# First seven input tiles of a two-layer expert kernel given a place each and issued from two queues

## The reference

```python
# layer 0, on x (8, 256, 1024)
base   = einsum('btd,od->bto', x, W)                    # W (1024, 1024)
logits = einsum('btd,ed->bte', x, Wr) + 5.0 * one_hot(language_ids)   # 8 experts
topw, topi = top_k(logits, 2)
gates  = sum(one_hot(topi, 8) * softmax(topw)[..., None], axis=-2)
h      = einsum('btd,erd->bter', x, A)                  # A (8, 16, 1024)
x      = x + base + 2.0 * einsum('bter,bte,eor->bto', h, gates, B)
# layer 1, on the new x
w      = weight[adapter_ids]                            # weight (16, 1024, 1024)
out    = x + einsum('bsi,boi->bso', x, w)
```

## Time and profile before

| | us |
|---|---|
| median of three runs | 405.21 (404.77 to 405.67) |
| the profiled execution's own time | 404.49 |
| span of the profiled execution | 402.7 |
| TensorE matmul busy | 396.1 (98%) |
| VectorE busy | 313.9 (78%) |
| ScalarE busy | 170.9 (42%) |
| GpSimd busy | 62.9 (16%) |
| DMA moved | 72.79 MB, mean 181 GB/s |

### The profile page before, as it was taken

The page is one execution under the profiler, slowest core; times in us unless marked ns, Lnnn a source line. Parts: engine busy times, 40 slices in busy tenths (PEclk is TensorE's granted clock), DMA queues, the critical chain, the costliest instruction groups (busy, mean ns, idle before and its releaser), DMA issues.

```text
span 402.7 us, 5968 instructions
## 1 busy us (share of the span) xinstructions
PE 396.1 (98%) x1920; PEld 334.6 (83%) x1920; DVE 313.9 (78%) x404; ACT 170.9 (42%) x231; POOL 62.9 (16%) x88
## 2 busy tenths in 40 slices
PE   8999999999999999999999999999998999999996
PEld 8999888888889888888888888888887887888884
DVE  2999999997457468329887958997979999999900
ACT  1443342754220143335355335465445566556511
POOL 1016102200000100000110222312313131314100
PEclk9999999999999999999999999999999999999999
DMA  7978520133376300007595999999999999999231
GB/s 188 232 200 221 151 61 0 53 106 104 115 215 207 92 0 2 1 0 206 127 297 211 311 249 302 266 304 284 261 284 269 286 277 302 292 263 271 66 104 52
DMA packets 78577, 72.79 MB, mean 181 GB/s; under 512 B 7090, under 2 KB 77266, under 8 KB 77522
## 3 DMA queue, kind: packets, MB, share of 16 engines
q1 hardware_dynamic: 51584, 47.21, 46.8%
q10 hardware_dynamic: 26962, 25.21, 19.9%
HBM read 55.61 MB, written 16.78 MB: 180 GB/s over the span
## 4 chain that ended last, share of the span: by engine, by line
PE 98%; issue 0%; POOL 0%; ACT 0%; POOLq 0%
PE banks L1178 15%; PE banks L1180 14%; PE banks L1179 14%; PE banks L1083 13%; PE banks L1081 13%; PE banks L1082 13%; PE banks L1074 7%; PE banks L1062 3%; PE banks L1092 2%; PE banks L1094 2%; PE banks L1093 2%; PE banks L1152 1%; PE banks L1101 0%; ACT sums L959 0%; POOL sums L415 0%
## 5 line engine op out<-in xcount | busy, mean ns | idle before, releaser
L1081 PE MATMUL banks<-ring,weights 128*128 128x512 f32 x192 | 75.0, 391 | 0.0
L427 POOL TENSOR_TENSOR raw<-raw,ident 128x128 f32<-128x128 f32 x50 | 34.9, 698 | 221.6 <-DMA raw<-in_L_cond_weight_dram 198.1
L1178 PE MATMUL banks<-weights,tokens 128*128 128x512 f32 x176 | 68.6, 390 | 0.0
L1180 PE MATMUL banks<-weights,tokens 128*128 128x512 f32 x176 | 68.5, 389 | 0.0
L1179 PE MATMUL banks<-weights,tokens 128*128 128x512 f32 x176 | 68.5, 389 | 0.0
L948 ACT ACTIVATE weights<-weights_f 128x1024 fp32r<-128x1024 f32 x44 | 46.5, 1060 | 50.1 <-DVE weights_f L634 46.5
L634 DVE STREAM_TRANSPOSE weights_f<-raw 128x1024 f32<-128x1024 f32 x42 | 51.8, 1235 | 10.5 <-POOL raw L427 10.0
L640 DVE TENSOR_TENSOR weights<-weights_f,weights 128x1024 fp32r<-128x1024 f32 x44 | 52.6, 1197 | 1.0 <-ACT weights L948 0.9
L1083 PE MATMUL banks<-ring,turned_w 128*128 128x512 f32 x128 | 49.8, 389 | 0.0
L1082 PE MATMUL banks<-tokens,weights 128*128 128x512 f32 x128 | 49.8, 389 | 0.0
L1081 PEld LDWEIGHTS banks<-ring,weights 128*128 128x128 f32 x192 | 36.0, 188 | 7.5
(11 more groups left out here) (116 smaller groups left out, 632.4 us busy)
## 6 DMA issues: line engine op xcount, KB each, us to landing
raw<-in_L_cond_weight_dram SPq DMA_DIRECT2D x168, 128.0 KB, 6.2
ring_f<-in_L_cond_weight_dram SPq DMA_DIRECT2D x88, 128.0 KB, 6.3
raw<-in_x_dram SPq DMA_DIRECT2D x64, 128.0 KB, 3.3
x_kept<-stage ACTq DMA_DIRECT2D x32, 256.0 KB, 4.1
out_dram<-sums ACTq DMA_DIRECT2D x32, 256.0 KB, 7.0
raw<-in_L_cond_W_dram SPq DMA_DIRECT2D x32, 128.0 KB, 3.1
sums<-x_kept ACTq DMA_DIRECT2D x3, 1024.0 KB, 7.4
stage<-x_kept ACTq DMA_DIRECT2D x3, 1024.0 KB, 9.7
```

What stands on the lines that cost most here:

```text
L427: nc.gpsimd.tensor_tensor(spot, spot, ident[:].rearrange("p (q j) -> p q j", q=Q), ALU.add)\
L1081: nc.tensor.matmul(ps, u_hi, x_hi, start=first and k == 0, stop=False, skip_group_check=True)
L1178: nc.tensor.matmul(l1_bank(o), x_hi, w_hi, start=m == 0, stop=False)
L1180: mm = nc.tensor.matmul(l1_bank(o), x_lo, w_hi, start=False, stop=m == M - 1)
```

## The change

`FRONT = 7`: the first seven tiles (A, x0 to x3, W0, W1) get places 0 to 6, of which 0 to 2 are in `raw` and 3 to 6 in `ring_f`. None of them waits. All later tiles of layer 0 go through the three places of `raw`, counted from the eighth tile; the w1 tiles' places are shifted accordingly. The four DMAs of each of the seven tiles are divided: parts 0 and 1 are issued by SyncE, parts 2 and 3 by ScalarE, ahead of, between and behind ScalarE's DMAs of Wr, the language ids and the adapter ids. On VectorE, the low part of W0 comes ahead of the transposition of W1.

```diff
+    FRONT = 7
+    SLOT = {item: k if k < FRONT else (k - FRONT) % RAW for k, item in enumerate(LOADS)}
     for n in range(NW1):
-        SLOT["w1", n] = (N_LOADS + n) % RAW if n < EARLY else (n - EARLY + RAW) % RAW1
+        SLOT["w1", n] = (N_LOADS - FRONT + n) % RAW if n < EARLY else (n - EARLY + RAW) % RAW1
...
+        def fill(engine, item, rows, parts=range(Q)):
+            s = SLOT[item]
+            for c in parts:
+                engine.dma_start(raw_tile(s)[c * S:(c + 1) * S, :].rearrange("p (q j) -> p q j", q=Q),
+                                 rows[:, :, c * DQ:(c + 1) * DQ]).then_inc(raw_loaded[s], 16)
...
             def load_w1(n):
                 item = ("w1", n)
-                if BEFORE[item]:
+                if BEFORE[item] in LOADS[:FRONT]:
+                    sp.wait_ge(steps, product_end(1, 3))
+                else:
                     sp.wait_ge(transposed, TURN_AT[BEFORE[item]] + 1)
-                else:
-                    sp.wait_ge(steps, product_end(1, 3))
...
-            for item in LOADS:
+            for item in LOADS[:FRONT]:
+                fill(sp, item, rows_of(item), (0, 1))
+            for item in LOADS[FRONT:]:
                 load(item)
...
             turn(("w", 0))
             low(("xt", 3))
+            low(("wt", 0))
             turn(("w", 1))
-            low(("wt", 0))
             turn(("w", 2))
...
         def _(act):
+            for item in LOADS[:2]:
+                fill(act, item, rows_of(item), (2, 3))
             act.wait_ge(wr_zeroed, 1)
             for c in range(Q):
                 act.dma_start(wr_raw[c * S:c * S + E, :], wr[:, c * DQ:(c + 1) * DQ]).then_inc(wr_loaded, 16)
+            for item in LOADS[2:4]:
+                fill(act, item, rows_of(item), (2, 3))
             act.dma_start(lang_i[:], lang_ids.partition_broadcast(P)).then_inc(lang_loaded, 16)
+            for item in LOADS[4:FRONT]:
+                fill(act, item, rows_of(item), (2, 3))
             act.dma_start(adapters[:], adapter_ids.unsqueeze(0)).then_inc(adapters_loaded, 16)
```

More of the change, by code:

```diff
@@ L72, in cond_resid_kernel @@
     N_LOADS = len(LOADS)
-    SLOT = {item: k % RAW for k, item in enumerate(LOADS)}
+    FRONT = 7
+    SLOT = {item: k if k < FRONT else (k - FRONT) % RAW for k, item in enumerate(LOADS)}
     for n in range(NW1):
-        SLOT["w1", n] = (N_LOADS + n) % RAW if n < EARLY else (n - EARLY + RAW) % RAW1
+        SLOT["w1", n] = (N_LOADS - FRONT + n) % RAW if n < EARLY else (n - EARLY + RAW) % RAW1
     ALL_LOADS = LOADS + [("w1", n) for n in range(NW1)]
@@ L78, in cond_resid_kernel @@
     FILLS, BEFORE = {}, {}
-    for s in range(RAW1):
+    for s in range(FRONT):
         here = [item for item in ALL_LOADS if SLOT[item] == s]
@@ L273, in cond_resid_kernel @@
         logits, top, hot1, hot2, gates = (scratch(k) for k in range(5))
-        raw_loaded = [sem(f"raw_loaded{s}") for s in range(RAW1)]
+        raw_loaded = [sem(f"raw_loaded{s}") for s in range(FRONT)]
         wr_loaded = sem("wr_loaded")
@@ L371, in l1_bank, with rows_of @@
             return banks[:, (o + 4) % 8, :]
+        def fill(engine, item, rows, parts=range(Q)):
[3 more added lines that the diff above has]
+                                 rows[:, :, c * DQ:(c + 1) * DQ]).then_inc(raw_loaded[s], 16)
+        def rows_of(item):
+            if item[0] == "a":
+                return a_rows[:, :].rearrange("(q s) d -> s q d", s=S)
+            if item[0] == "x":
+                t0 = item[1] * 2 * HALF + item[2] * HALF + item[3] * P
+                return x_rows[t0:t0 + P, :].rearrange("(q s) d -> s q d", s=S)
+            return w0.rearrange("(q m s) d -> m s q d", m=M, s=S)[item[1]]
         block = ctx.enter_context(nc.Block())
@@ L376, in _ @@
         def _(sp):
[L377 to L381, removed]
             def load(item):
@@ L389, in load @@
                                      b_pairs[c]).then_inc(raw_loaded[SLOT[item]], 16)
[L390 to L394, removed]
                 else:
-                    fill(item, w0.rearrange("(q m s) d -> m s q d", m=M, s=S)[item[1]])
+                    fill(sp, item, rows_of(item))
             def load_w1(n):
                 item = ("w1", n)
-                if BEFORE[item]:
+                if BEFORE[item] in LOADS[:FRONT]:
+                    sp.wait_ge(steps, product_end(1, 3))
+                else:
                     sp.wait_ge(transposed, TURN_AT[BEFORE[item]] + 1)
-                else:
-                    sp.wait_ge(steps, product_end(1, 3))
-                fill(item, w1_rows[bass.ds(ids[n // M] * D, D), :].rearrange("(q m s) d -> m s q d", m=M, s=S)[n % M])
-            for item in LOADS:
+                fill(sp, item, w1_rows[bass.ds(ids[n // M] * D, D), :].rearrange("(q m s) d -> m s q d", m=M, s=S)[n % M])
+            for item in LOADS[:FRONT]:
+                fill(sp, item, rows_of(item), (0, 1))
+            for item in LOADS[FRONT:]:
                 load(item)
```

## The result

The change makes the kernel slower by 0.4%: 406.0 us (median of 22 runs, 404.22 to 409.51) against 404.79 (22 runs, 403.08 to 405.94) for the kernel before in the same comparison. The ratio is 1.0042 with a 95% interval of 1.0022 to 1.0061, some 1.7 us, of which the interval allows 0.9 to 2.5. The forecast was no change, 405.2.

The account below looks back on a forecast made before the run. TensorE was taken as the bound, its two identity blocks setting when the first product starts. The change's parts summed as 0 + 0 + 0 + 0, so the forecast stayed at the median, 405.2 us, range 404.6 to 406.0.

Parts of the forecast that it names:

- The bound: Front: TensorE's two identity blocks set the first product's start; VectorE's low part before the product at 53.98 has 0.39 us room.
- s: Start of x0's low part on VectorE: 11.66 us before, forecast 12.0 to 13.8; from 13.85 on the change would lose time.
- Earlier loads ... costs 0 and brings 0: Front: A about 0.3 us and W0 about 1 us earlier, all beside the identity block that ends at 14.5, so 0.
- the change doesn't do what it says: Rival on the front: DMA engines are full, tiles land no earlier, time equals the forecast; counted there, no chance of its own.
- a shared descriptor generator: Rival, the two queues take turns: 0.93 us an issue for each, 4.7 us past the point, 409.9 us; chance 0.09.
- If all of that idle time can be caught up: s up to 13.85: VectorE's stretch 11.66 to 53.59: its 1.8 us idle plus 0.39 us room would absorb a later start of x0's low part.
- The price of an issue: ScalarE's fourteen added DMAs in the front: 0.59 us each, just below the 0.60 from which time is lost, so 0.
- the rival that I held for the likeliest way to lose: ScalarE held up by its own dense issues, x0's high part late: 407.0 us at 0.72 an issue, 408.9 at 0.86; chance 0.24.
- W0's low part first, 0: VectorE's reorder: W0's low part ends 1.17 us earlier, but TensorE doesn't come for it before 24.52, so 0.
- Wr and the ids, 0: Front: Wr's DMAs 1.9 us later with 4.6 to spare, language ids issued at about 6.3 and wanted at 13, so 0.
- Tile 11, 0: Layer 1: tile 11 is issued up to 1.65 us later; taken as 0. As a rival 406.9 us, chance 0.05.
- Faster, if the stop of layer 1 goes: Rival: shifted places bring tiles 12 and 13 earlier and remove TensorE's 1.3 us stop, 403.9 us; chance 0.07.

Follow-up runs that it names:

- e10: The change, but ScalarE issues halves of A, x0 and x1 alone and SyncE issues the rest whole, without a wait: ratio to the kernel before 1.0018.
- e13: The change with one wait added: SyncE issues its halves of x2 and later only when the A tile is transposed; ratio to the kernel before 1.0001.
- e8: The changed kernel measured once more against the kernel before: ratio 1.0040 (1.0007 to 1.0073).
- e9: The change without the reorder on VectorE (W1's transposition again ahead of W0's low part): ratio to the kernel before 1.0012.
- e11: The kernel before with halves of A, x0 and x1 issued by ScalarE and W0's low part ahead of W1's transposition: ratio 1.0001.
- e5: The kernel before with only VectorE's reorder, W0's low part ahead of W1's transposition: median 406.41 us against 404.13, ratio 1.0027.
- e3: The change with seven places in the front, but later tiles in the places they had in the kernel before: ratio to that kernel 1.0012.
- e1: The kernel before with w1 tile 11 waiting for tile 8's transposition, as in the change: ratio 1.0012.
- e6: The kernel before with parts 2 and 3 of A, x0 and x1 issued by ScalarE, three places and orders unchanged: ratio 0.9999.
- e7: The kernel before with halves of A, x0 and x1 issued by ScalarE and w1 tile 11 waiting for tile 6: ratio 0.9993.
- e12: The same kernel as e6, measured a second time against the kernel before: ratio 0.9993.
- e14: The kernel of e10 with SyncE's loads of x2 and later held until the A tile is transposed: ratio to the kernel before 1.0007.
- e4: The change with all four parts of the seven tiles issued by SyncE and ScalarE's list as before: ratio to the kernel before 1.0028.

## Why the prediction was wrong

**The bound: right in the place, wrong in its kind.** The tightest place was named, VectorE's last low part ahead of the product at 54, and the loss is there. The room was misread: the 53.98 of the earlier trace rows is not the product's first matmul, which starts at 53.82, so there were 0.23 us and not 0.39, and the limit for s is 13.69 and not 13.85. That the length of the identity block is "a count in the code" is wrong too: its end moves by 1.6 us among the profiles.

**"Earlier loads ... costs 0 and brings 0": this step failed.** It saw that the DMA engines set the pace, and counted their bytes as if they came in the order in which the tiles are wanted. With full engines a tile that is asked for earlier pushes another back. When x1 was in, the engines had moved 2.42 MB for the two queues in the change and 1.97 in before (counted from the trace's packets), for tiles of which the first three hold 1.57. The rival "the change doesn't do what it says" had the tiles land no earlier; none had one land later. The Trainium skill, in DMA: Bandwidth & Descriptors, "Queues, rings and completion order", says that each DMA engine goes round the queues that have work, a packet at a time. The trace of e10 agrees from 3 to 5 us, where each queue moved 0.27 MB. From 6 to 8.5 us it was 0.47 MB for SyncE's and 0.13 for ScalarE's, which even turns alone don't give; why SyncE's got more stays open. I had drawn another sentence of that section (a shared descriptor generator) into a rival, and that one didn't come true: fourteen issues took 0.54 us each, not 0.93.

**"If all of that idle time can be caught up: s up to 13.85": this step failed too.** s was 13.12, inside the limit, and the last low part came 1.5 us later than before. From s to the end VectorE's stretch was 41.93 us before, 42.00 in the change, and 41.17 in e13:

```profile
12.25:53.42 41.17, 41.17 (x265) 37.06 (x264) 40.24 (x48) 16.54 (x24) 10.44 (x12) 1.00 0.78 192
```

Of the 1.8 us of idle time, nothing to 0.8 could be had. Two things kept it. Late tiles brought waits of their own, 0.58 us for W0 among them (it landed at 19.20; at 17.41 in before and 17.69 in e8). In all 1.14 us of the stretch were idle. And VectorE's instructions became slower, 0.74 us in all; the rows point to GpSimd, beside which it now runs where it had waited for it. The change, VectorE and then GpSimd:

```profile
40.37 0.91 DVE L504 TENSOR_TENSOR ring<-weights_f,ring 128x512 fp32r<-128x512 f32 x1
41.21 0.94 DVE L526 TENSOR_TENSOR weights_f<-tokens_f 128x512 f32<-128x512 f32 x1
```

```profile
39.46 1.28 POOL L445 TENSOR_TENSOR tokens_f<-tokens_f 128x512 f32<-128x512 f32 x1 [0.72 <-PE banks L1088]
40.70 0.90 POOL L435 TENSOR_TENSOR raw<-raw,ident 128x128 f32<-128x128 f32 x1
```

and the first of the two in before, a low part that GpSimd's instruction overlaps in its last 0.03 us only (the next one of GpSimd starts at 39.34, behind it):

```profile
39.19 0.65 DVE L496 TENSOR_TENSOR ring<-weights_f,ring 128x512 fp32r<-128x512 f32 x1
```

0.65 us becomes 0.91. From 37 to 45 us the change has six such instructions and before two. VectorE's busy time in the stretch rose from 40.12 to 40.86 us, for the same list. The Trainium skill, SBUF — State Buffer, "SBUF: two separate sides", says that VectorE and GpSimd share a pair of ports, and that an instruction of VectorE with two inputs locks it against GpSimd, whichever starts first. The trace agrees that the two slow each other: at 40.37 GpSimd's instruction has 0.37 us to go, and VectorE's takes 0.26 longer than alone. That the ports are the place no run here shows.

**The price of an issue: right mechanism, near size, wrong judge.** 0.59 us was taken, 0.54 measured (start to start, with waits inside), and ScalarE ended at 10.7 where 11.5 was allowed. It does delay x0's low part, by 0.36 us in the change and 0.61 in e13. But e10 takes it away and is slowest in the front, and e13 keeps it and is as before: it was not what decided. So the rival that I held for the likeliest way to lose had the right sign for a wrong reason.

**W0's low part first, 0: right** for the change (e9 and e11; e5 leaves a doubt where there are three places). **Wr and the ids, 0: nearly**: VectorE waits 0.74 us for Wr, but x1 is what ends the wait behind it; in e3 it also waited 0.37 us for the language ids, at 13.9. **Tile 11, 0: right as far as can be told** (e1, and S in the table). **Faster, if the stop of layer 1 goes:** the stop is no fixed thing to lose. I had read 1.3 us in one execution as a property of the kernel; S goes from 0 to 5.8 us among executions of kernels that are the same there.

**What would be seen.** Foretold: table load 9.7 to 11.5 (10.74), x0's low part 12.0 to 13.8 (13.12), W0's low part over by 23 (23.58, wrong), features at 14.5 (13.29 in the change, and 13.00 to 14.57 in the others, so the start that I took for fixed is not). And "the loss is then to be read as the start of that product less 53.98": the right place, but it gives 1.25 and 0.57 for the two profiles of the change, and 53.82 gives 1.41 and 0.73.

## What to carry to other kernels

With the DMA engines full, free places and a second queue made nothing faster here; they changed the order in which the bytes came. Before you let a queue run ahead, ask which tile is wanted next and on which queue each part of it stands: the split of a tile brought it earlier (A landed at 4.9 to 5.3 in e6, e7, e11 and e12, at 5.5 to 6.1 where it wasn't split), but x1 only when the other queue was held back until then, here by one wait. Not even that made the kernel faster than before. And idle time of an in-order engine is not a reserve until you have asked what it waited for; if that was an engine with which it then collides, part of it comes back as slower instructions.

## What was not expected of the hardware

- **Stops of 0 to 5.8 us in layer 1** in kernels that are alike there, with the DMA engines at a share near 1.0. By the sum above they can make up most of the spread of single runs (402.6 to 409.1 us for the kernel before), and a difference of 0.3% can't be read from one profile.
- **TensorE's clock behind a stop.** Behind the stop of 2.54 us at 267.9 in the change the granted clock was 0.65 over the next 3.5 us, 1.74 us of time above the pace. In e14 it stayed at 1.00 behind a longer one, 3.4 us. What tells them apart stays open:

```profile
269.00:273.00 4.00, 3.97 (x17) 3.30 (x18) 4.00 (x4) 2.73 (x4) 1.18 (x2) 1.00 1.00 310
```

- **A tile 3.6 us behind its neighbour at full rate.** In e4 and e6, W1 landed 3.6 us after W0 (3.4 in e9), though the DMA engines moved their usual 230 GB/s meanwhile. A transfer of 16 KB on the instruction queue (q8) stands at about 15 to 17 us in both, but e8 has it as well, at 16.0, and its tiles land 2.0 to 2.3 us apart. Open.
